# A recommender tower on one core: chunks in four steps instead of six, products two samples wide in two rounds

## The reference

```python
x = layer_norm(dense_t @ Wd.T, gd, bd)                       # (B, 128)
y = layer_norm(einsum('bnd,ed->bne', e, Ws), gs, bs)         # per gathered row
y = layer_norm(einsum('bne,pn->bep', y, Wsi), gsi, bsi)      # 26 rows -> 32, per sample
T = concatenate([x[:, None, :], swapaxes(y, 1, 2)], axis=1)  # 33 vectors of 128
Z = einsum('bnd,bmd->bnm', T, T)                             # products of all pairs
z = (layer_norm(Z[:, TRIL_I, TRIL_J] @ Wl.T, gl, bl) * mask)
h = concatenate([z, dense_t], axis=1)
h = maximum(h @ W_top1 + b_top1, 0); h = maximum(h @ W_top2 + b_top2, 0)
y = h @ W_top3
```

## Time and profile before

| | |
|---|---|
| median of 3 runs | 614.19 us (613.42 to 615.02) |
| the profiled execution, its own device time | 615.38 us |
| its span | 613.6 us |
| PE busy (matmul) | 529.8 us, 86% |
| PE weight loads | 376.2 us, 61% |
| DVE busy | 435.1 us, 71% |
| ACT busy | 259.3 us, 42% |
| GpSimd busy | 395.9 us, 65%, last gather at 525.6 us |

### The profile page before, as it was taken

The page is one execution under the profiler, slowest core; times in us unless marked ns, Lnnn a source line. Parts: engine busy times, 40 slices in busy tenths (PEclk is TensorE's granted clock), DMA queues, the critical chain, the costliest instruction groups (busy, mean ns, idle before and its releaser), DMA issues.

```text
span 613.6 us, 15555 instructions
## 1 busy us (share of the span) xinstructions
PE 529.8 (86%) x6347; PEld 376.2 (61%) x6347; DVE 435.1 (71%) x807; ACT 259.3 (42%) x629; POOL 395.9 (65%) x420
## 2 busy tenths in 40 slices
PE   1466788778789999999999999999999999998877
PEld 1353565465556766666667676767667666755645
DVE  3396689778875797679877886779767976795110
ACT  1113155444343554354544554445544543544212
POOL 5777777777777777777777777777777777200000
PEclk9997789989999999999999999999999999999998
DMA  7911113121212131212222131313121212010100
GB/s 235 366 26 27 27 28 59 36 49 28 58 28 58 29 76 27 57 30 52 50 41 45 30 74 28 59 27 75 30 58 27 58 29 58 13 31 9 24 1 0
DMA packets 28566, 31.65 MB, mean 52 GB/s; under 512 B 9928, under 2 KB 20944, under 8 KB 28112
## 3 DMA queue, kind: packets, MB, share of 16 engines
q0 software_dynamic: 13312, 13.66, 12.4%
q1 hardware_dynamic: 15168, 16.99, 10.5%
q10 hardware_dynamic: 16, 0.01, 0.0%
HBM read 23.28 MB, written 0.01 MB: 38 GB/s over the span
## 4 chain that ended last, share of the span: by engine, by line
PE 54%; POOL 21%; issue 12%; ACT 8%; DVE 4%; DMA 1%; ACTq 0%; SPq 0%
POOL emb L262 21%; PE bank_h L391 11%; PE bank_m L414 10%; PE bank_u L358 8%; PE bank_y L369 5%; PE bank_m L442 5%; PE bank_z L379 4%; PE bank_t L334 3%; ACT zt L627 2%; ACT zbig L578 2%; PE bank_g L344 2%; DVE ssum L831 1%; PE bank_m L449 1%; ACT h L636 1%; ACT embt L551 1%
## 5 line engine op out<-in xcount | busy, mean ns | idle before, releaser
L262 POOL DMA_INDIRECT emb<-in_tables,ids x416 | 395.7, 951 | 130.4 <-issue 122.9
L561 ACT COPY us<-bank_u 128x512 f32<-128x512 f32 x64 | 37.5, 586 | 166.4 <-PE bank_u L358 166.4
L831 DVE TENSOR_REDUCE ssum<-sq 128x32 f32<-128x1024 f32 x64 | 77.8, 1216 | 38.3 <-ACT sq L566 37.2
L391 PE MATMUL bank_h<-wz,zr 128*128 128x512 f32 x224 | 104.0, 594 | 0.6 <-ACT zt L627 0.6
L358 PEld LDWEIGHTS bank_u<-mix_w,emb 128*128 128x128 f32 x512 | 84.8, 204 | 26.9 <-DVE emb L814 15.8
L358 PE MATMUL bank_u<-mix_w,emb 128*128 128x192 f32 (+4 forms) x512 | 89.9, 323 | 11.9 <-DVE emb L814 11.8
L825 DVE TENSOR_TENSOR tt<-bank_y,biasc 128x512 f32<-128x512 f32 x128 | 81.4, 678 | 0.0
L369 PE MATMUL bank_y<-us,proj 64*128 64x512 f32 x256 | 75.8, 666 | 5.4 <-DVE tt L825 5.2
L840 DVE TENSOR_TENSOR tt<-tt,bank_g 128x1024 f32<-128x1024 f32 x64 | 78.1, 1220 | 2.2
L566 ACT ACTIVATE sq<-tt 128x1024 f32<-128x1024 f32 x64 | 68.8, 1075 | 12.6 <-DVE tt L825 12.3
L334 PEld LDWEIGHTS bank_t<-eye,emb 128*128 128x128 f32 x208 | 22.9, 147 | 76.5 <-issue 43.1
(11 more groups left out here) (107 smaller groups left out, 523.4 us busy)
## 6 DMA issues: line engine op xcount, KB each, us to landing
emb<-in_tables,ids POOLq DMA_INDIRECT x416
zs<-zbig SPq DMA_DIRECT2D x64, 70.0 KB
zs<-zbig SPq DMA_DIRECT2D x64, 42.0 KB
dense<-in_dense SPq DMA_DIRECT2D x8, 256.0 KB, 4.5
wfull<-in_wfull SPq DMA_DIRECT2D x1, 2048.0 KB, 10.0
wz<-in_wrows SPq DMA_DIRECT2D x1, 1792.0 KB, 13.6
w<-in_w SPq DMA_DIRECT2D x1, 1280.0 KB
w<-in_w SPq DMA_DIRECT2D x1, 512.0 KB
```

The lines of the kernel that those rows point to most:

```text
L262: pool.indirect_dma_start(emb[:, e, t, D * a:D * a + D], None, x_in["tables"], bass.IndirectOffsetOnAxis(ap=ids[:, col:col + 1], axis=0),) ...
L391: mm = pe.matmul(bank_h[:, :], zr[:, s, :], wz[:, s, :], start=(s == 0), stop=(s == SLOTS - 1))
L831: dve.tensor_reduce(ssum[:, h % 2, :], sq[:, :, :], AX.X, ALU.add).then_inc(ssum_ok, 1)
```

## The change

- Lags: a chunk goes through `turn`, `gram` and the row scaling and `mix`, `project` and the normalization, `products` in four successive steps (lags 1 to 4) instead of lags 2 to 7 (8 for `products_out`). Everything that follows per unit or super has its lag cut by 4. The loop has 77 steps.
- Order on PE: project, gram, products round 0, pieces of top1 and flat, products round 1, top3, top2, the dense work, turn_z, mix, turn.
- Order on DVE: `scale_e` ahead of `sum_s`. On ACT: `rows_out` directly behind `mixed_out`; then `squares` first half, `products_out` round 0, `root_e`, `squares` second half, `products_out` round 1, `root_s`.
- `products`: 16 matmuls, each of two samples: 64 wide and 68 columns long, in two column groups; half of what they form is not used. They come in two rounds of 8, and `zbig`, `products_out` and the addresses of the moving DMAs follow that. `squares` and `products_out` become two instructions per chunk.
- GpSimd waits on `turned` and, in the middle of each chunk's gathers, on `z_done`.
- The late preparation of `wz` is spread over one more step.
- At the end: the last unit's moving DMAs are split between SyncE and ACT, and the last super's three layers run as two halves of 128 samples.

The diff, cut to its core (the late preparation, the tail's bodies and renamed indices are left out):

```diff
+HALVES = ((0, 2), (2, 4)), ((4, 6), (6, 7)), ((7, 9), (9, 10)), ((10, 12), (12, 13))
+WIDE = 2
+TILE = PR * WIDE
+ROUNDS = ((0, 4), (4, 8))
+NR = len(ROUNDS)
...
-TURN_AT, GRAM_AT, SCALE_AT, MIX_AT, PROJ_AT, CHAIN_AT, PROD_AT, ZOUT_AT = 2, 3, 4, 4, 5, 6, 7, 8
-XCOL_AT, MOVE_AT, FLAT_AT, TURNZ_AT, GAINZ_AT = 6, 11, 13, 16, 17
-DENSEX_AT, TURNX_AT, SUMX_AT = 1, 2, 3
-TOP1_AT, TOP2_AT, TOP3_AT = (22, 23, 24), 28, 29
+TURN_AT, GRAM_AT, SCALE_AT, MIX_AT, PROJ_AT, CHAIN_AT, PROD_AT, ZOUT_AT = 1, 2, 2, 2, 3, 3, 4, 4
+XCOL_AT, SUMCOL_AT, MOVE_AT, FLAT_AT, TURNZ_AT, GAINZ_AT = 2, 3, 7, 9, 12, 13
+TOP1_AT, TOP2_AT, TOP3_AT = (18, 19, 20), 24, 25
 LAST = NSUP - 1
-OPEN_AT, CLOSE_AT = 8 * LAST + 17, 8 * LAST + 21
-STEPS = CLOSE_AT + 4
+TAIL = 8 * LAST + 8
+LAST1_AT, LAST2_AT, LAST3_AT = (TAIL + 5, TAIL + 9), (TAIL + 8, TAIL + 10), (TAIL + 9, TAIL + 11)
+RELU1_AT, RELU2_AT = (TAIL + 6, TAIL + 10), (TAIL + 9, TAIL + 11)
+STEPS = TAIL + 13
...
-        tt = sb("tt", [P, 2, UNIT, ZC])
+        tt = sb("tt", [P, 2, UNIT // WIDE, ZC, WIDE])
-        zbig = sb("zbig", [P, 2, CZ, 32])
+        zbig = sb("zbig", [P, 2, WIDE, CZ, 32])
...
                     after(pool, mixed, 4 * (u - EB) + min(c + 2, 4))
-                    after(pool, grammed, 4 * u + c - 3)
+                    after(pool, turned, 4 * u + c - 2)
+                    for part, (t0, t1) in enumerate(HALVES[c]):
+                        if part == 1:
+                            after(pool, z_done, NR * (4 * u + c - 5) + 1)
...
-                for j in range(4):
+                for j in range(4 if u < NU - 1 else 2):
...
                 pe.wait_ge(embt_ok, 4 * u + k + 1)
-                after(pe, t_ok, 4 * u + k + GRAM_AT - CHAIN_AT + 1)
-                after(pe, scaled, 4 * u + k + GRAM_AT - SCALE_AT + 1)
+                after(pe, scaled, 4 * u + k)
...
+            def products(u, h, i):
+                if i == 0:
+                    pe.wait_ge(t_ok, 4 * u + h + 1)
+                    pe.wait_ge(xcol_ok, u + 1)
+                after(pe, zc_ok, NR * (4 * u + h) + i)
+                g0, g1 = ROUNDS[i]
+                for g in range(g0, g1):
+                    for q in range(4 // WIDE):
+                        o = ZC * WIDE * (g - g0)
+                        some = tt[:, u % 2, 4 // WIDE * (8 * h + g) + q, :, :].rearrange("p c w -> p (c w)")
+                        mm = pe.matmul(bank_z[TILE * q:TILE * q + TILE, o:o + ZC * WIDE],
+                                       some[:, C0 * WIDE:ZC * WIDE], some, start=True, stop=True)
                 mm.then_inc(z_done, 1)
...
             for s in range(STEPS):
-                c = chunk(s, PROD_AT)
-                if c:
-                    products(*c)
                 c = chunk(s, PROJ_AT)
                 if c:
                     project(*c)
-                c = chunk(s, TURN_AT)
+                c = chunk(s, GRAM_AT)
                 if c:
-                    turn(*c)
+                    gram(*c)
+                pd = chunk(s, PROD_AT)
+                if pd:
+                    products(*pd, 0)
...
+                if pd:
+                    products(*pd, 1)
...
-                c = chunk(s, GRAM_AT)
+                c = chunk(s, TURN_AT)
                 if c:
-                    gram(*c)
+                    turn(*c)
...
-            def squares(u, h):
+            def squares(u, h, a):
+                act.wait_ge(y_ok, 2 * (4 * u + h) + a + 1)
...
+                pj, se, pd = chunk(s, CHAIN_AT), chunk(s, SCALE_AT), chunk(s, ZOUT_AT)
+                if pj:
+                    squares(*pj, 0)
+                if pd:
+                    products_out(*pd, 0)
+                if se:
+                    root_e(*se)
+                if pj:
+                    squares(*pj, 1)
+                if pd:
+                    products_out(*pd, 1)
+                if pd == (NU - 1, 3):
+                    move_rest()
+                if pj:
+                    root_s(*pj)
                 u = unit(s, XCOL_AT)
                 if u is not None:
                     xcol(u)
+                u = unit(s, SUMCOL_AT)
+                if u is not None:
                     place_sum_x(u)
...
             def scale_t(u, h):
                 dve.wait_ge(sstd_ok, 4 * u + h + 1)
-                after(dve, prod_ok, min(4 * u + h + CHAIN_AT - SCALE_AT + 1, 4 * NU))
-                srs = bank_g[:, 0:2 * GRP]
+                after(dve, zc_ok, NR * (4 * u + h))
+                srs = bank_z[:, 512 - 2 * GRP:512]
```

More of the change, by code:

```diff
@@ L107, in sup, with x_of, top1_of @@
     return c // 8 if c >= 0 and c % 8 == 0 and c // 8 < NSUP else None
-def top1_of(s, piece):
-    j = sup(s, TOP1_AT[piece])
-    return j if j is not None and j < LAST else None
+def x_of(s, part):
+    if s == part:
+        return 0
+    i = sup(s, part - 3)
+    return i if i else None
+def top1_of(s, part):
+    if s == TAIL + (2, 2, 3)[part]:
+        return LAST - 1
+    j = sup(s, TOP1_AT[part])
+    return j if j is not None and j < LAST - 1 else None
 def top2_of(s):
-    if s == CLOSE_AT + 1:
-        return LAST
-    if s == OPEN_AT:
+    if s == TAIL + 4:
         return LAST - 1
@@ L130, in top3_of, with gains_z_of, half_of @@
     return j if j is not None and j < LAST - 1 else None
+def gains_z_of(s):
+    if s == TAIL + 4:
+        return NU - 2
+    u = unit(s, GAINZ_AT)
+    return u if u is not None and u != NU - 2 else None
+def half_of(s, steps):
+    return steps.index(s) if s in steps else None
 def dlrm(nc, x_in, out):
@@ new lines, in last1 @@
+            def last1(a):
+                cols = slice(UNIT * a, UNIT * a + UNIT)
+                pe.wait_ge(zt_ok, NU - 1 + a)
+                if a == 0:
+                    pe.wait_ge(scaled, 4 * NU)
+                for c in range(4):
+                    if a == 0:
+                        o, first = bank_g[:, UNIT * c:UNIT * c + UNIT], (3, 4)
+                    else:
+                        o, first = last_banks[c][:, 0:UNIT], ()
+                    for t in first + (0, 1, 2):
+                        rhs = zt[:, t, cols] if t < 3 else dense[:, LAST % DB, t - 3, cols]
+                        mm = pe.matmul(o, w1[:, t, P * c:P * c + P], rhs, start=(t == 3), stop=(t == 2))
+                    if a == 1:
+                        mm.then_inc(last_done, 1)
+                if a == 0:
+                    mm.then_inc(top1_done, 1)
@@ new lines, in last2 @@
+            def last2(a):
+                cols = slice(UNIT * a, UNIT * a + UNIT)
+                pe.wait_ge(h1_ok, 2 * LAST + 1 + a)
+                if a == 0:
+                    pe.wait_ge(y_out, LAST)
+                else:
+                    pe.wait_ge(h2_ok, LAST + 1)
+                for c in range(2):
+                    for t in range(4):
+                        mm = pe.matmul(bank_m[:, UNIT * c:UNIT * c + UNIT], w2[:, t, P * c:P * c + P],
+                                       h1[:, t, cols], start=(t == 0), stop=(t == 3))
+                mm.then_inc(top2_done, 1)
@@ L436, in top2, with last3 @@
+            def last3(a):
+                cols = slice(UNIT * a, UNIT * a + UNIT)
+                pe.wait_ge(h2_ok, LAST + 1 + a)
+                pe.wait_ge(t_ok, 4 * NU)
+                pe.wait_ge(zc_ok, 4 * NR * NU)
+                for c in range(2):
+                    mm = pe.matmul(bank_z[0:1, cols], w3c[:, c:c + 1], h2[:, c, cols],
+                                   start=(c == 0), stop=(c == 1))
+                mm.then_inc(top3_done, 1)
             def top2(j):
@@ L665, in _ @@
                     mixed_out(*c)
-                c = chunk(s, ZOUT_AT)
+                c = chunk(s, GRAM_AT)
                 if c:
-                    products_out(*c)
-                u = unit(s, GAINZ_AT)
-                if u is not None:
+                    rows_out(*c)
+                u = gains_z_of(s)
+                if u is not None and u != NU - 2:
                     gains_z(u)
```

283 lines of the change are left out of this document (149 added, 134 removed).

## The result

The changed kernel takes 659.01 us (658.30 to 659.10 in four runs) against 613.81 for the one before on the same chip: a ratio of 1.0736, interval 1.0708 to 1.0764. The forecast was 621.7 us, slower by 1.2%, with a range of 600 to 634. The sign was right; the size was not, and the time lies outside the range.

A forecast was written before the change was run, and what follows sets the result against it. Gathers were taken to bound the head to 147.65 us, then PE's circle at 70.25 per eight steps, to 550.9; a tail of 70.2 gave a span of 621.1 and a median of 621.7 us, range 600 to 634.

The forecast's parts named there:

- The circle: Each step runs mixed_out, project, gram, products, fill, products, mix; eight steps sum to 70.25 us against 65.39 before.
- M: A step's mark at mixed_out, from which steps are counted; project's first load was forecast 0.70 us behind it.
- step 0: Step with s modulo 8 = 0: products round 1 waits 0.75 us for round 0's copy; 9.57 us in all.
- steps 6 and 7: Steps with little fill, by s modulo 8: ACT's root_s and copies hold up mixed_out; 8.25 and 7.45 us.
- GpSimd's waits: The new waits in the gathers cost nothing, since gathers run ahead by nearly two steps and follow PE.
- Gathers still set the head: Up to step 18 gathers set the pace; with flat alone as fill, PE takes about 65 us for eight steps.
- M(18): Mark of step 18, where the gather-bound head ends: forecast at 147.65 us.
- products: On PE, the wider products take 0.50 us a round, 1.0 a chunk, between bounds of 0.39 and 1.22.
- Rival B: Products cost 0.40 us a round or less, root_s does not hold up mixed_out: 601 us; chance 0.34.
- rival C: PE loses 0.23 us at each of three more array shape changes a step, 4.2 per eight: 646 us; chance 0.07.
- squares: On ACT, half a chunk's squares take 0.65 us, from 1.075 for a whole chunk.
- the tail: From step 64's mixed_out to the end 70.2 us; from the last chunk's turn some 61 in place of 79.

The follow-up runs named there:

- f5: s3 with project and all behind it one step later, mixed_out staying, and GpSimd's waits looser: 596.70 us, ratio 0.9698.
- s2: The changed kernel with squares written in the order they are read, sum_s reading with a stride of two: 652.35 us, ratio 1.0626.
- h4: The changed kernel without GpSimd's two new waits: 657.20 us, ratio 1.0696.
- g1: The changed kernel with the late preparation of wz left out, so that values differ: 640.54 us.
- s1: The changed kernel with products one sample wide again, still in two rounds: 637.78 us, ratio 1.0373.
- s3: The changed kernel with products one sample wide, all 32 in one round ahead of the fill: 619.43 us, ratio 1.0073.
- e3: The changed kernel with products one sample wide in one round, on the chip where the kernel before took 1009.53 us: 916.88 us.
- e2: The changed kernel with squares written in the order they are read, on the chip where the kernel before took 1009.53 us: 796.97 us.
- e4: The changed kernel without GpSimd's two new waits, on the chip where the kernel before took 1009.53 us: 971.72 us.

## Why the prediction was right and wrong

**Right.** The circle: that a step runs from mixed_out over project to mix, that project starts right behind M (0.62 to 0.64 us, 0.70 forecast), that step 0 waits for the copy between its rounds, and that in steps 6 and 7 ACT's root_s and copies hold up mixed_out (for step 6 the rows ahead of 355.68 above; it is little, 0.13 us over the 1.40 from mix, which began at 354.15). The circle is shown by f5, which takes project out of the circle and gains 3.05 us per eight steps. Step 0's wait, in the timeline:

```profile
365.99 1.12 ACT L641 ACTIVATE sq<-tt 128x512 f32<-128x512 f32 x1 [0.28 <-issue]
...
366.90 0.43 ACT L654 COPY zbig<-bank_z 128x272 f32<-128x272 f32 x1
...
367.39 0.55 PEld L411 LDWEIGHTS bank_z<-tt 128*64 128x64 f32 x16 [0.96 <-issue]
```

PE stood 0.81 us there (0.75 forecast). Round 1 began 4.07 behind M(40) at 363.32, for 3.85 forecast, and round 0's end was later by nearly as much. That the wait's size came out is luck: squares took 1.12 and not the 0.65 of the forecast, and in s2, where they take 0.63, PE stands only 0.48. GpSimd's waits cost nothing, as said (h4).

**Wrong, the largest: "Gathers still set the head."** I asked only whether flat leaves PE within the gathers' pace, found 65 us against 65.04, and took that for enough. A stage without slack holds its pace but never makes good a delay, and the late preparation is a delay of 17 to 18 us. It stood in the change (it goes from steps 4 to 7 to steps 3 to 8, so over two more steps and not one), and I did not cost it. 18.2 of the 36.1 us are lost here, 17.3 of them by the late preparation (g1: M(18) 148.54). The rest of the sentence is wrong too: PE waits for no gather in the head, with the late work or without it, and that g1 comes within 0.9 of my 147.65 is in part luck, a pace of PE's own that lies close to the gathers'. Nor does the kernel before stop waiting for gathers at chunk 16, as I read it; turn of chunk 20 still waits 1.89 us, at 180.81.

**Wrong in size: products.** I took 0.50 a round, 1.0 for the chunk, between bounds of 0.39 and 1.22 for it; it is 0.62, so 1.25, just above my upper bound. Per column group 16 pairs of load and matmul took 1.25 us, 78 ns each, where 68 columns stream in 57; the old form has 48 for 29. A fixed part of about 20 ns stayed with each pair; my 1.0 left room for 6. Nor is there a floor at which 34 and 68 columns cost alike. Rival B's premise, that half the instructions cost half the time, is refuted: half the instructions cost 1.6 times as much.

**Wrong in size: changes of the array's shape (rival C).** The two changes around the fill cost 0.2 us together (4.07 for 3.88 above), about 0.1 each. For steps 2 to 4 my sum had none of it, and rival C had up to 0.23 for each of three changes more. The second round as a whole, its changes and step 0's wait together, costs 1.30 us per eight steps (s1 to s3), so C's kind of loss is there, at less than a third of its 4.2. The Trainium skill, TensorEngine Tiling, Key Properties, says that a change of tiling mode drains the engine; the 0.1 us a change agree with that in kind.

**Wrong: squares.** I had half a chunk at 0.65 from the row of a whole one. It took 1.115, since the change writes the results of a pair of samples in turn, 32 floats apart; in the order of reading it takes 0.626 (s2), and sum_s, reading with a stride of two floats, stays at 1.211. It costs only 0.44 us per eight steps. The Trainium skill, SBUF — State Buffer, Door 1: The DMA port swizzle, has lines of 16 bytes and a penalty for each access that goes to a new one; 0.63 against 1.115 us for 512 columns agrees with it, and so does the free stride of two floats.

**Wrong: the tail, 8.7 us.** Five terms of it in the timeline:

```profile
608.77 0.69 PE L411 MATMUL bank_z<-tt 128*64 128x68 f32 x16 [2.35 <-DVE tt L960]
609.39 2.04 PE L446 MATMUL bank_m<-dense,w 128*128 128x256 f32 x4
...
611.22 2.28 PE L446 MATMUL bank_m<-zt,w 128*128 128x256 f32 x6
...
618.46 2.78 ACTq L752 DMA_DIRECT2D zs<-zbig  x4
621.29 0.84 ACT L715 ACTIVATE h<-bank_m,vecs 128x256 f32<-128x256 f32 x2 [2.85 <-issue]
...
622.18 5.41 PE L505 MATMUL bank_m<-h,w 128*128 128x256 f32 x16 [4.17 <-ACT h L715]
```

Steps 64 and 65 took 0.6 us more. Step 67's products wait 2.35 for scale_t, which stands behind root_s, that behind products_out of round 1, and that behind 6 us of fill: a chain that I had followed in the mid-run and not here. The four DMA issues on ACT took 2.78, with the relu that top2 needs behind them, so from round 1's end to top2 PE stood 4.2 where I had 2.3 for copy, issues and relus (1.9 more). And PE came back slow after both waits, 1.8 and 1.95 more: the granted clock was 0.68 from 608 to 612, behind 2.35 us of idling, and 0.72 from 622 to 628, behind 4.17, where 1.00 is the 2.4 GHz level. Busy time and granted clock of PE in those stretches:

```profile
608.00:612.00 4.00, 3.23 (x22) 0.68 0.02 4
...
622.00:628.00 6.00, 5.74 (x19) 0.72 0.05 11
```

The sum is 8.6. Nearly all of the 1.8 belongs to this execution and not to the wait: in h4's, PE waits the same 2.35 us, keeps 1.00, and top1's ten records take 2.26 from start to start (610.18 to 612.44), not 3.95 as here (609.39 to 613.34):

```profile
609.55 0.69 PE L408 MATMUL bank_z<-tt 128*64 128x68 f32 x16 [2.35 <-DVE tt L957]
610.18 1.13 PE L443 MATMUL bank_m<-dense,w 128*128 128x256 f32 x4
611.14 1.46 PE L443 MATMUL bank_m<-zt,w 128*128 128x256 f32 x6
612.44 1.03 PE L443 MATMUL bank_m<-dense,w 128*128 128x256 f32 x4
```

Behind the wait of 4.2 top2 took 5.25 us from start to start in h4 as well. In s3, with one round, PE has neither wait, and the same top2 takes 3.45 (586.09 to 589.54).

## What to carry to other kernels

When a change shortens a pipeline, write down for each step the circle that begins and ends at the same instruction, and ask how much slack the step keeps against whatever feeds it: a stage that only just keeps pace pays in full for every delay ahead of it. Here 17.3 us at chunk 7 were still 17.5 at chunk 63, where the kernel before had made good 10.1 us by chunk 10. A result that is copied and used in the same step puts its handoff into that circle; one lag more for it gave 3 us per eight steps and, with narrow products in one round, the fastest kernel of this study, 596.70 us. And count a matmul form by its pairs per column group, with their columns and a fixed part, not by its instructions.

## What the runs showed that was not expected

On one chip the kernel before took 1009.53 us, and the changed kernel's variants between 796.97 and 971.72, with the same durations of squares and sum_s. In e3 there, PE's loads of products came in small bunches with gaps that nothing released:

```profile
380.30 0.15 PEld L411 LDWEIGHTS bank_z<-tt 128*32 128x32 f32 x3 [0.61 <-issue]
381.03 0.11 PEld L411 LDWEIGHTS bank_z<-tt 128*32 128x32 f32 x1 [0.57 <-issue]
381.74 0.17 PEld L411 LDWEIGHTS bank_z<-tt 128*32 128x32 f32 x5 [0.61 <-issue]
```

It looks as if instructions reached the engines late. Their number does not order the totals: e2 and e4 have as many matmuls as each other and took 796.97 and 971.72. What was wrong on that chip was not tested.
